# Half norms of a routed feed-forward query taken from its first product, with every engine's order of steps laid out anew

## The chip, the cores and the metric

The kernel runs on one core of one Trainium2 chip. The metric is the device time of one execution in microseconds (us). Before the change it was 1391.68 us, the median of 3 runs (1388.91 to 1394.45).

## The reference, cut to what matters

The input is 16 sequences of 375 steps with 64 channels. One layer is computed: a convolution over 9 steps with a norm-dependent scale and tanh (367 steps of 128 features are left), a banded attention with three window widths, and a feed-forward part that picks experts by product keys. The change is in the last:

```python
q = (hn @ Wq.T + bq).reshape(b, s, 8, 64)             # 8 heads of 64
mu, var = mean(q, -1), mean((q - mu) ** 2, -1)
q = (q - mu) / sqrt(var + 1e-5) * ln_g + ln_b
q0, q1 = q[..., :32], q[..., 32:]                     # two halves a head
s0 = l2norm(q0) @ l2norm(keys0).T                     # 64 keys each
s1 = l2norm(q1) @ l2norm(keys1).T
# top 16 of each, top 16 of the sums of pairs, softmax, experts ix0 + ix1
out = sum(gelu(hn . down[expert]) * w * up[expert])
```

So each tile needs, for each head, the variance of q and the squared norms of the two halves of the normalised q.

## The kernel before, in words

A sequence (batch) is worked in three tiles of 124 positions, t = 0, 1, 2. Each engine has a function `body(c)` that holds, in an order written out by hand, the steps it does in round c. The steps of a round belong to up to four batches: `do(step, c + k, t)` does the step for batch c + k, and nothing if there is no such batch. Engines meet through counting semaphores alone; every engine works strictly in the order of its own body. There are 20 rounds, c = -2 to 17. In `run`, rounds -2 to 3 are written out, rounds 4 to 13 are a hardware loop of five turns with two rounds each, and rounds 14 to 17 are written out again.

The steps around the change, for one tile:

- `q_product` (TensorE): q of the tile in bankQ, 124 positions x 512, one product of 512 columns plus a bias product from three rows (`fbq3`).
- `q_squares` (ScalarE): 8 squares with a running sum, one per head, give the variance (`qss`).
- `q_std` (GpSimd): adds eps, takes the root with a power, splits it in three bf16 parts (`std3`), and makes the guard. `q_turn_std` (TensorE) turns the parts, `q_stdT` (ScalarE) copies them.
- `q_second` (TensorE): a second product, with the gain in the weights (`wgT`) and the turned deviation times the bias: q times its deviation, 124 x 512 again.
- `q_norms` (ScalarE): 16 squares with a running sum, one per half, give `nss`. `q_guard` (VectorE) takes the larger of norm and guard, `q_scale` (GpSimd) its power -0.5.
- `q_score` (TensorE) computes 1024 key scores, `q_scores` (ScalarE) copies them, `rank` (VectorE) finds the top 16 of 16 x 64 values in four steps and two halves of the heads, `rank_sums` (GpSimd) adds pairs into 50 cells a head, `choose` (VectorE) takes the top 16 of these, and `mark`, `select`, `normalise`, `turn_cells`, `merge_cells`, `one_high`, `one_low`, `low_weights`, `scatter`, `product`, `experts_out`, `finish` turn them into the output of the tile.

Steps whose names begin with `p1_` are the convolution and attention of a later batch. `q_inner` and `q_gelu` (four each per batch) compute the experts' activations.

Set-up work stands in the first rounds: `turn_weights` (TensorE, round -1) waits for all feed-forward loads (`ffn_in`, L429), `key_norms`, `centred_weights`, `bias_parts` (VectorE, round -1) and `split_bias` (round 0) prepare weights and biases, `key_products` (TensorE, round 0) multiplies keys into weights, `send_parts` (the SP queue, L446) moves nine pieces of bias, and `copy_parts` (ScalarE, L734) copies them once they have landed. In VectorE's body the first step of a round is `p1_res` (L1434) and the second `product` (L1508).

Of the kernel before, what the change touches and what calls it, by code (L numbers as in the profile page):

```python
# [66 lines left out]
def build(nc, x, tok_kernel, tok_bias, wq, bq, wk, bk, wo, bo, gamma, beta, fwq, fbq, lng, lnb,  # L67
          keys0, keys1, down, up, merge, ident, own, out):
# [4 lines left out]
    with ctx:  # L73
# [21 lines left out]
        own_sb = sb("own_sb", [128, TG])  # L95
        ones = sb("ones", [128, 128])
        ones3 = sb("ones3", [3, NT], bf16)
# [129 lines left out]
        bankM = ctx.enter_context(nc.psum_tensor("bankM", [128, 1024], f32))  # L227
        wcT_ps = bankS[0:2 * NC, :].bitcast(f16).rearrange("p (k n) -> p k n", k=2)
# [10 lines left out]
        setup_fbq, fbq_spread = sem("setup_fbq"), sem("fbq_spread")  # L239
# [44 lines left out]
        qss_ready = sem("qss_ready")  # L284
# [3 lines left out]
        q2_done = sem("q2_done")  # L288
# [89 lines left out]
        def run(eng, start, body, end):  # L378

            start()  # L380
            for b in range(BEFORE, PEELED):
                body(Batch(b // 2, b % 2))
            with eng.Fori(PEELED // 2, B // 2 - 1) as j:
                body(Batch(j, 0))
                body(Batch(j, 1))
            for b in range(B - 2, AFTER):
                body(Batch(b // 2, b % 2))
            end()
# [10 lines left out]
                     (own_sb[:, :], own), (merge_sb[:, :], merge)]  # L399
# [6 lines left out]
        def _(sp):  # L406
# [24 lines left out]
            def spread():  # L431
# [3 lines left out]
                sp.wait_ge(setup_fbq, 5)  # L435
                for k in range(2):
                    sp.dma_start(fbq3[1 + k:2 + k, :], fbq_part[0:1, k, :]).then_inc(fbq_spread, 16)
# [11 lines left out]
            def body(c):  # L449
                if not at(c, -2):  # L450
                    do(load_x, c + 2)
                if at(c, -1):
                    spread()
                if at(c, 0):
                    send_parts()
                do(store, c + -2, 0)
# [12 lines left out]
        def _(pool):  # L469
# [226 lines left out]
        def _(act):  # L696
# [227 lines left out]
            def body(c):  # L924
# [47 lines left out]
                if at(c, -1):  # L972
                    copy_parts()
# [703 lines left out]
```

## Time and profile before

| | |
|---|---|
| median of 3 runs | 1391.68 us (1388.91 to 1394.45) |
| profiled execution | 1389.55 us, span 1387.7 us |
| VectorE (DVE) | 1284.9 us busy, 93% |
| TensorE (PE) | 1029.8 us, 74% |
| GpSimd (POOL) | 940.4 us, 68% |
| ScalarE (ACT) | 919.2 us, 66% |
| granted TensorE clock | 0.759 of full speed, mean |

The span is the time from the first to the last instruction of the profiled execution; what lies around it is 1.85 us. A busy time counts overlapping instructions of an engine once. "Idle before" is the time in which the engine did nothing before an instruction, with the instruction whose semaphore released it; "issue" means that no semaphore explains the wait. Because engines work in order, one late step delays all behind it on its engine.

### The profile page before, as it was taken

The page shows a single profiled execution, that of the slowest core. Times are in us where ns is not written, and L with a number is a line of the kernel's source. Part 1 is how long each engine was busy: PE and PEld are TensorE (multiplying, and loading weights), DVE is VectorE, ACT ScalarE, POOL GpSimd, SP SyncE. Part 2 cuts the span into 40 slices and gives each one's busy share as a digit, 9 for nine tenths or more (in the row PEclk, how much of TensorE's full clock was granted, in tenths as well). Part 3 has the DMA queues.
Part 4 walks back from the last instruction along what each step waited for, and adds up shares of the span by engine and source line. Part 5 has one row for each costly group of instructions (what it writes and reads, how often), then busy time and mean ns, then how long its engine had stood idle before and what let it go on. Part 6 is the DMA issues. An engine that isn't in the chain of part 4 may idle for free.

```text
span 1387.7 us, 41186 instructions
## 1 busy us (share of the span) xinstructions
PE 1029.8 (74%) x9585; PEld 679.4 (49%) x9585; DVE 1284.9 (93%) x10050; ACT 919.2 (66%) x4155; POOL 940.4 (68%) x1947
## 2 busy tenths in 40 slices
PE   4767777877777777778778777786778878776753
PEld 2434554645455454555446454553545545463433
DVE  4349999999999989999899998999999999999995
ACT  2576867668586857858576784767658676766532
POOL 4438776786867768577677867676776777668552
PEclk7787786769788776878877696787868778685555
DMA  2100000000000000000000000000000000000000
GB/s 55 18 15 2 3 11 3 4 8 6 10 4 11 4 5 11 4 10 4 12 4 5 9 6 10 4 12 3 5 9 5 6 3 5 4 4 5 3 4 7
DMA packets 22512, 10.97 MB, mean 8 GB/s; under 512 B 13920, under 2 KB 22032, under 8 KB 22242
## 3 DMA queue, kind: packets, MB, share of 16 engines
q1 hardware_dynamic: 21618, 7.79, 2.5%
q8 instruction: 82, 1.34, 0.4%
q14 instruction: 188, 1.54, 0.4%
q10 hardware_dynamic: 624, 0.30, 0.1%
HBM read 4.58 MB, written 3.01 MB: 5 GB/s over the span
## 4 chain that ended last, share of the span: by engine, by line
DVE 60%; issue 15%; PE 8%; ACT 7%; POOL 6%; SPq 1%; DVEq 1%; DMA 0%; POOLq 0%; ACTq 0%
DVE idx L1466 14%; DVE val L1464 9%; DVE cr L1536 8%; DVE scores L1469 8%; DVE oh L1479 6%; DVE best L1534 4%; DVE wl L1499 3%; ACT ns_junk L863 2%; PE banks L1055 2%; DVE bns L1389 2%; DVE masked L1419 1%; POOL cs L623 1%; PE bankM L1219 1%; PE bankQ L1142 1%; ACT act_g L840 1%
## 5 line engine op out<-in xcount | busy, mean ns | idle before, releaser
L1466 DVE FIND_INDEX8 idx<-val,scores 124x8 uint16<-124x64 f32 x1536 | 304.4, 216 | 0.0
L1464 DVE MAX8 val<-scores 124x8 f32<-124x64 f32 x1536 | 210.6, 207 | 2.4 <-ACT scores L870 1.2
L1219 PE MATMUL bankM<-wl,oh 128*128 128x16 f16 x5952 | 162.8, 172 | 46.2 <-DVE wl L1499 46.2
L1219 PEld LDWEIGHTS bankM<-wl,oh 128*128 128x128 f16 x5952 | 160.0, 101 | 59.6 <-DVE wl L1499 33.2
L597 POOL TENSOR_TENSOR qscale<-nmx,power 124x16 f32<-124x16 f32 x48 | 147.8, 3079 | 45.4 <-DVE nmx L1443 45.3
L1469 DVE MATCH_REPLACE8 scores<-val,scores 124x64 f32<-124x64 f32 x768 | 151.4, 206 | 0.0
L863 ACT ACTIVATE ns_junk<-bankQ 124x32 f32<-124x32 f32 x768 | 138.0, 255 | 12.7 <-PE bankQ L1172 12.4
L1479 DVE TENSOR_SCALAR oh<-eh 128x992 f16<-128x992 int16 x384 | 135.2, 414 | 4.5 <-ACT eh L918 4.5
L863 ACT ACTIVATION_READ_ACCUMULATOR ns_junk<-bankQ 124x1 f32 x768 | 138.3, 268 | 0.0
L1108 PE MATMUL banks<-diag,probs 124*124 124x124 f32 x672 | 107.7, 327 | 25.0 <-ACT diag L808 25.0
L1227 PE MATMUL bankM<-up_x,prod 128*124 128x128 f32 x384 | 86.5, 396 | 50.5 <-DVE prod L1508 50.5
L900 ACT ACTIVATE wcell<-wn 124x400 f16<-124x400 f32 x48 | 27.0, 562 | 142.0 <-POOL wn L648 142.0
L1108 PEld LDWEIGHTS banks<-diag,probs 124*124 124x124 f32 x672 | 100.3, 235 | 37.1 <-ACT diag L808 31.1
L1227 PEld LDWEIGHTS bankM<-up_x,prod 128*124 128x124 f32 x384 | 74.5, 287 | 76.8 <-DVE prod L1508 72.3
L623 POOL TENSOR_TENSOR cs<-val_s 124x64 f32<-124x64 f32 (+4 forms) x480 | 103.8, 250 | 7.5
L1466 DVE MATCH_VALUE_LOAD idx<-val,scores 124x8 f32 x1536 | 108.2, 70 | 0.0
L1182 PE MATMUL bankS<-wgk,hnT 128*124 128x512 f32 x192 | 105.3, 631 | 0.0
L1142 PE MATMUL bankQ<-hnT,down_x 128*128 128x372 f32 x128 | 74.0, 668 | 38.7 <-ACT ns_junk L863 22.4
L849 ACT ACTIVATE sq_junk<-bankQ 124x64 f32<-124x64 f32 x384 | 79.4, 238 | 31.6 <-PE bankQ L1156 31.3
L561 POOL TENSOR_TENSOR sbias<-smax,minus_scale 124x3 f32<-124x3 f32 x48 | 9.3, 195 | 133.0 <-DVE smax L1419 133.0
L1155 PE MATMUL bankQ<-fwqT,hnT 128*124 128x512 f32 x96 | 77.9, 905 | 14.5 <-ACT hnT L830 14.3
L586 POOL TENSOR_TENSOR std<-qvar,power 124x8 f32<-124x8 f32 x48 | 79.2, 1649 | 3.8
(196 smaller groups left out, 3067.8 us busy)
## 6 DMA issues: line engine op xcount, KB each, us to landing
x_in<-in_x SPq DMA_DIRECT2D x16, 93.8 KB
x_in<-in_x SPq DMA_DIRECT2D x16, 62.5 KB
out<-o_sb SPq DMA_DIRECT2D x16, 62.0 KB
out<-o_sb SPq DMA_DIRECT2D x16, 61.0 KB
out<-o_sb SPq DMA_DIRECT2D x16, 60.5 KB
x_in<-in_x SPq DMA_DIRECT2D x16, 31.0 KB
oh<-more SPq DMA_DIRECT2D x6, 54.0 KB
conv_w<-in_L_tok_kernel ACTq DMA_DIRECT2D x2, 128.0 KB, 3.2
```

The source lines that it names most:

```text
L597: g.tensor_tensor(qscale[c.slot(t)][:, :, :].rearrange("p h s -> p (h s)"), nmx[:, :, :].rearrange("p h s -> p (h s)"), power[0:NT, 0, :], ...
L623: g.tensor_tensor(dst[:, :, at:at + m], src[:, :, 0, a:a + 1].to_broadcast([NT, k, m]), src[:, :, 1, 0:m], ALU.add)
L863: last = a.activation(ns_junk[:, i, :], bankQ[0:NT, i * HALF:(i + 1) * HALF], ACT.Square, accum_out=nss[:, i // 2, i % 2:i % 2 + 1])
L1108: last = e.matmul(bankB[0:NT, k * NT:(k + 1) * NT], probs[t][w][:, OFF[k]:OFF[k] + NT], diag[:, w, :], start=w == windows[0], stop=w == wi ...
L1182: e.matmul(part, hnT[c.par][:, t, :], wgk[:, 2 * k:2 * k + 2, :].rearrange("p k n -> p (k n)"), start=True, stop=False)
L1219: last = e.matmul(coef[:, g, :, :], oh[:, k, g, :, :].rearrange("p v t -> p (v t)"), wl[:, part, k, :, TG * g:TG * (g + 1)], start=k + par ...
L1227: last = e.matmul(ffn, prod[:, l, :], up_x[:, l, :], start=l == 0, stop=l == EL - 1)
L1464: last = v.max(out=v_[:, hd, s, best8], in_=src[:, hd, s, :])
L1466: last = v.max_index(out=i_[:, hd, s, best8], in_max=v_[:, hd, s, best8], in_values=src[:, hd, s, :])
L1469: last = v.match_replace(out=src[:, hd, s, :], in_to_replace=v_[:, hd, s, best8], in_values=src[:, hd, s, :], imm_value=NEG)
L1479: last = v.tensor_scalar(by_shift[:, :, :, value, :], eh[:, :, :, :].rearrange("p s k (g t) -> p s (k g) t", t=TG), float(value), None, AL ...
L1536: last = v.match_replace(out=cr[:, hd, :], in_to_replace=best[:, hd, best8], in_values=left[:, hd, :], imm_value=NEG)
```

## The change

`q_product` gives q turned: four products with 128 rows of weights each, so that two heads' features lie on the partitions and the 124 positions are the columns. `q_squares` squares these four pieces, with the centred bias added on the way in (`q_lin[:, 16+k]`). A short product with six columns of weights then gives sums of the squares: two for the variances and four for the half norms, weighted with the gain squared. What is missing of a half norm is linear in q and in the deviation; `q_linear` computes it from four more weights per pair of heads (`q_lin[:, 0:16]`, and the first 16 columns of `bias96`). `q_nss` multiplies that by the deviation and adds it. A small matrix of block sums (`blocks`), the gain and the bias as columns are loaded: five loads more. `key_products` gets twelve short products, and the bias in three bf16 parts (`fbq3`, its two sends and five operations) goes.

The hardware loop goes: all 20 rounds are written out. The bodies of all engines are laid out anew.

```diff
         def run(eng, start, body, end):
             start()
-            for b in range(BEFORE, PEELED):
-                body(Batch(b // 2, b % 2))
-            with eng.Fori(PEELED // 2, B // 2 - 1) as j:
-                body(Batch(j, 0))
-                body(Batch(j, 1))
-            for b in range(B - 2, AFTER):
+            for b in range(BEFORE, AFTER):
                 body(Batch(b // 2, b % 2))
             end()
...
-                     (own_sb[:, :], own), (merge_sb[:, :], merge)]
+                     (own_sb[:, :], own), (blocks_sb[:, :], blocks), (merge_sb[:, :], merge)]
+        for i in range(2):
+            ffn_loads += [(gain_col[i * QD:(i + 1) * QD, :], col(lng)), (bias_col[i * QD:(i + 1) * QD, :], col(lnb))]
...
         # GpSimd
             def q_std(c, t):
...
-                link(g.tensor_tensor(qvar[:, :], qss[:, :], eps8[:, :], ALU.add))
...
+            def q_nss(c, t):
+                n = c.tile(t)
+                link = linker(pool, nss_ready, 2, n)
+                pool.wait_ge(sums_ready, n + 1)
+                pool.wait_ge(std_ready, 4 * n + 1)
...
+                link(g.tensor_tensor(by_pair(nlin[:, :, :]), lin, std, ALU.mult))
+                link(g.tensor_tensor(by_pair(nss[:, :, :]), by_pair(nlin[:, :, :]), squares, ALU.add), wait=False)
         # ScalarE
             def q_squares(c, t):
...
-                for i in range(H):
-                    last = a.activation(sq_junk[:, i, :], bankQ[0:NT, i * QD:(i + 1) * QD], ACT.Square, scale=QD ** -0.5, accum_out=qss[:, i:i + 1])
+                for k in range(PAIRS):
+                    last = a.activation(sqT[:, k * NT:(k + 1) * NT], bankQ[:, k * NT:(k + 1) * NT], ACT.Square, bias=q_lin[:, 16 + k:17 + k])
...
+            def q_var(c, t):
...
+                a.activation(qvar[:, :].rearrange("p (k h) -> p k h", h=2), q_sums_ps[:, :, 0:2], ACT.Identity, bias=eps8[:, 0:1]).then_inc(qvar_ready, 1)
...
-            def q_norms(c, t):
-                for i in range(2 * H):
-                    last = a.activation(ns_junk[:, i, :], bankQ[0:NT, i * HALF:(i + 1) * HALF], ACT.Square, accum_out=nss[:, i // 2, i % 2:i % 2 + 1])
+            def q_halves(c, t):
...
+                a.activation(half_sums[:, :, :], q_sums_ps[:, :, 2:10], ACT.Copy).then_inc(sums_ready, 1)
         # TensorE
             def q_product(c, t):
...
-                e.matmul(bankQ[0:NT, :], hnT[c.par][:, t, :], fwqT[:, :], start=True, stop=False)
-                e.matmul(bankQ[0:NT, :], ones3[:, :], fbq3[:, :], start=False, stop=True).then_inc(q_done, 1)
+                for k in range(PAIRS):
+                    last = e.matmul(bankQ[:, k * NT:(k + 1) * NT], fwqT[:, k * 128:(k + 1) * 128], hnT[c.par][:, t, :], start=True, stop=True)
+                last.then_inc(q_done, 1)
+            def q_sums(c, t):
+                n = c.tile(t)
+                pe.wait_ge(squared, n + 1)
+                for k in range(PAIRS):
+                    last = e.matmul(bankQ[0:NT, 10 * k:10 * k + 6], sqT[:, k * NT:(k + 1) * NT], q_sum_w[:, 0:6], start=True, stop=True)
+                last.then_inc(qsum_done, 1)
...
-            def q_second(c, t):
-                e.matmul(bankQ[0:NT, :], hnT[c.par][:, t, :], wgT[:, :], start=True, stop=False)
-                e.matmul(bankQ[0:NT, :], std96T[:, :], bias96[:, 0:H * QD], start=False, stop=True).then_inc(q2_done, 1)
+            def q_linear(c, t):
...
+                e.matmul(q_sums_ps[:, :, 6:10], hnT[c.par][:, t, :], by_pair(q_lin[:, 0:16]), start=True, stop=False)
+                e.matmul(q_sums_ps[:, :, 6:10], std96T[:, :], by_pair(bias96[:, 0:16]), start=False, stop=True).then_inc(lin_done, 1)
```

The new orders, where the prediction speaks of them (only the steps named):

```
TensorE, before:  ... p1_conv(c+1), p1_sum_sq(c+1), [round -1: turn_weights], q_turn_std(c-1,2) ...
TensorE, after:   ... [round -1: turn_weights], q_turn_std(c-1,2), q_linear(c-1,2), merge_cells(c-1,0), p1_conv(c+1), p1_sum_sq(c+1) ...
SP, before:       load_x(c+2), [round -1: spread], [round 0: send_parts], stores
SP, after:        [round -1: spread], [round 0: send_parts], load_x(c+2), stores
ScalarE, before:  ... q_squares(c+1,0), [round -1: copy_parts], ..., q_stdT(c+1,0), p1_ln(c+2,0), q_norms(c+1,0), [round -1: q_scores(0,0)], q_gelu(c+1,0), p1_xlT(c+2), ... q_gelu(c+1,1), ..., p1_qk(c+2) ...
ScalarE, after:   ... q_squares(c+1,0), best_exps(c,1), [round -1: copy_parts], mark(c,1), q_var(c+1,0), cell_exp(c,1), q_stdT(c+1,0), q_halves(c+1,0), ..., p1_ln(c+2,0), q_gelu(c+1,0), p1_xlT(c+2), ... q_gelu(c+1,1), ..., p1_qk(c+2), [round -1: q_scores(0,0)] ...
GpSimd, before:   rank_sums(c,0,0), rank_sums(c,0,1), ... normalise(c,2)
GpSimd, after:    q_nss(c,1), rank_sums(c,0,0), rank_sums(c,0,1), ... normalise(c,1), q_nss(c+1,0), ... normalise(c,2)
VectorE, before:  p1_res(c), product(c-2,2), p1_stats(c,1), ..., p1_moments(c,2), one_low(c-1,0), [round 0: split_bias], one_high(c-1,0), p1_shift(c,2), p1_wsq(c+1), ...,
                  rank(c-1,2,0,0), choose(c-1,1,0..3), ..., choose(c-1,2,0..3), one_high(c-1,1,0), p1_smax(c+1,0), one_low(c-1,1), one_high(c-1,1,1), ..., sum_exps(c,0), rank(c,1,0,0), rank(c,1,0,1), invert_sums(c,0)
VectorE, after:   p1_stats(c,1), invert_sums(c-1,0), p1_moments(c,1), rank(c-1,1,0,1), product(c-2,2), ..., choose(c-1,1,0), p1_shift(c,2), [round 0: split_bias], p1_wsq(c+1), ..., one_high(c-1,0), choose(c-1,1,2..3), rank(c-1,2,0,0), ...,
                  choose(c-1,2,0..2), p1_smax(c+1,0), one_high(c-1,1,0), one_low(c-1,1), one_high(c-1,1,1), choose(c-1,2,3), low_weights(c-1,1), ..., low_weights(c-1,2), p1_res(c+1), rank(c,1,0,0)
VectorE, batch 0: before rank(0,0,0,0..3), ..., p1_smax(1,0), p1_rden(1,0), p1_smax(1,1), p1_rden(1,1), p1_smax(1,2), rank(0,0,1,0..3)
                  after  p1_smax(1,0), ..., rank(0,0,0,0..3), p1_rden(1,0), p1_smax(1,1), p1_smax(1,2), p1_rden(1,1), rank(0,0,1,0..3)
```

## Rows read from the trace of the kernel before

**Rows 1.** The page: busy us (share of the span) and instructions.
```profile
PE 1029.8 (74%) x9585; PEld 679.4 (49%) x9585; DVE 1284.9 (93%) x10050; ACT 919.2 (66%) x4155; POOL 940.4 (68%) x1947
```

**Rows 2.** By stretch: length; PE, PEld, DVE, ACT, POOL busy; clock, DMA, GB/s.
```profile
113.70:432.65 318.95, 246.39 (x2379) 164.40 (x2379) 314.07 (x2500) 226.88 (x1036) 232.35 (x477) 0.79 0.02 6
432.65:1087.06 654.41, 504.17 (x4777) 336.15 (x4776) 630.88 (x5002) 455.22 (x2072) 464.21 (x952) 0.77 0.03 7
1087.06:1245.20 158.14, 122.91 (x1193) 82.37 (x1191) 157.16 (x1252) 113.26 (x516) 113.34 (x235) 0.79 0.02 4
1245.20:1387.70 142.50, 86.84 (x967) 55.16 (x965) 125.61 (x956) 65.75 (x299) 77.56 (x168) 0.57 0.02 5
```

**Rows 3.** DVE's waits, 432.65 to 1087.06: us in total, times, longest.
```profile
DVE res L1434 <- issue: 8.6, 4, 2.3
DVE prod L1508 <- issue: 7.4, 4, 1.9
```

**Rows 4.** Groups of ACT: output<-input xcount | busy us, mean ns | idle before.
```profile
L863 ACT ACTIVATE ns_junk<-bankQ 124x32 f32<-124x32 f32 x768 | 138.0, 255 | 12.7 <-PE bankQ L1172 12.4
L849 ACT ACTIVATE sq_junk<-bankQ 124x64 f32<-124x64 f32 x384 | 79.4, 238 | 31.6 <-PE bankQ L1156 31.3
L900 ACT ACTIVATE wcell<-wn 124x400 f16<-124x400 f32 x48 | 27.0, 562 | 142.0 <-POOL wn L648 142.0
```

**Rows 5.** Groups of PE, the same columns.
```profile
L1108 PE MATMUL banks<-diag,probs 124*124 124x124 f32 x672 | 107.7, 327 | 25.0 <-ACT diag L808 25.0
L1155 PE MATMUL bankQ<-fwqT,hnT 128*124 128x512 f32 x96 | 77.9, 905 | 14.5 <-ACT hnT L830 14.3
```

**Rows 6.** Groups of POOL, the same columns: the power and the splits of `q_std`.
```profile
L586 POOL TENSOR_TENSOR std<-qvar,power 124x8 f32<-124x8 f32 x48 | 79.2, 1649 | 3.8
L589 POOL TENSOR_TENSOR std<-std 124x9 f32<-124x9 f32 x96 | 19.3, 201 | 7.5
```

**Rows 7.** POOL in order of time, beside `split_bias`: start us, us, instruction.
```profile
58.12 1.61 POOL L554 TENSOR_TENSOR lnv<-bna,eps 124x3 f32<-124x3 f32 x1 [1.25 <-DVE bna L1399]
```

**Rows 8.** PE and DVE in order of time, 8 to 29 us.
```profile
8.30 6.09 PE L1055 MATMUL banks<-xT,conv_w 128*128 128x367 f32 x10 [0.95 <-ACT xT_sq L742]
14.32 0.81 PE L1064 MATMUL banks<-ones,sq_win 128*124 128x1 f32 x6
16.78 0.16 DVE L1366 TENSOR_SCALAR wsq<-banks 124x3 f32<-124x3 f32 x1
27.57 1.59 PE L1087 MATMUL banks<-xlT,wq_sb 128*128 128x367 f32 x2 [0.57 <-ACT xlT L779]
```

**Rows 9.** SP's queue in order of time: two of the loads.
```profile
11.85 0.37 SPq L429 DMA_DIRECT2D merge_sb<-in_merge  x1
12.27 2.42 SPq L429 DMA_DIRECT2D up_x<-in_L_ffn_expert_up  x4
```

**Rows 10.** DVE's waits, 0 to 113.7: us in total, times, longest.
```profile
DVE rden L1427 <- ACT probs L799: 13.5, 5, 3.7
DVE key_sq L1313 <- DMA up_x<-in_L_ffn_expert_up: 7.3, 1, 7.3
```

**Rows 11.** DVE and ACT in order of time, 49 to 86 us.
```profile
49.19 0.56 DVE L1434 TENSOR_TENSOR res<-banks,xb 124x384 f32<-124x384 f32 x1 [0.85 <-DVE key_z L1351]
72.28 1.48 ACT L734 ACTIVATE bias<-oh 96x1536 bf16<-96x1536 bf16 x1 [2.56 <-DMA oh<-more]
80.86 1.11 DVE L1464 MAX8 val<-scores 124x8 f32<-124x64 f32 x8 [1.17 <-ACT scores L870]
85.46 0.59 ACT L788 ACTIVATE kT<-banks,bk_sb 128x367 f32<-128x367 f32 x1
```

**Rows 12.** DVE in order of time, the last tile.
```profile
1365.34 0.20 DVE L1548 RECIPROCAL wrec<-wsum 124x8 f32<-124x8 f32 x1
```

**Rows 13.** ACT and POOL in order of time, a batch outside the loop.
```profile
1143.11 0.27 ACT L856 ACTIVATE std96T<-bankQ 96x124 bf16<-96x124 f32 x1 [0.74 <-PE bankQ L1162]
1150.02 0.40 POOL L617 TENSOR_TENSOR val_s<-val,qscale 124x128 f32<-124x128 f32 x1 [1.12 <-DVE val L1464]
```

More of the change, by code:

```diff
@@ L67, in build @@
 def build(nc, x, tok_kernel, tok_bias, wq, bq, wk, bk, wo, bo, gamma, beta, fwq, fbq, lng, lnb,
-          keys0, keys1, down, up, merge, ident, own, out):
+          keys0, keys1, down, up, merge, ident, own, blocks, out):
     f32, f16, bf16, i16, u16 = mybir.dt.float32, mybir.dt.float16, mybir.dt.bfloat16, mybir.dt.int16, mybir.dt.uint16
@@ L671, in body @@
                 do(q_std, c + 1, 0)
+                do(select, c, 1)
                 do(p1_rstd, c + 2, 0)
-                do(select, c, 1)
-                do(q_scale, c, 2)
+                do(normalise, c, 1)
                 if at(c, -2):
@@ L677, in body @@
                     setup_ffn()
[L678 removed]
+                do(q_nss, c + 1, 0)
+                do(p1_xb, c + 2)
                 do(rank_sums, c, 2, 0)
                 do(rank_sums, c, 2, 1)
+                do(rank_sums, c, 2, 2)
+                do(q_scale, c + 1, 0)
                 do(p1_sbias, c + 2, 0)
[L682 to L684 removed]
+                do(select, c, 2)
                 do(p1_sbias, c + 2, 1)
@@ L975, in body @@
                     copy_weights()
+                do(mark, c, 1)
+                do(q_var, c + 1, 0)
                 do(cell_exp, c, 1)
-                do(best_exps, c, 1)
-                do(mark, c, 1)
                 do(q_stdT, c + 1, 0)
+                do(q_halves, c + 1, 0)
+                do(weight_high, c, 1)
                 do(p1_ln, c + 2, 0)
-                do(q_norms, c + 1, 0)
-                do(weight_high, c, 1)
-                if at(c, -1):
-                    q_scores(c + 1, 0)
                 do(q_gelu, c + 1, 0)
@@ L1597, in body @@
                 do(rank, c + -1, 2, 1, 3)
+                do(choose, c + -1, 2, 0)
+                do(choose, c + -1, 2, 1)
+                do(choose, c + -1, 2, 2)
+                do(p1_smax, c + 1, 0)
+                do(one_high, c + -1, 1, 0)
+                do(one_low, c + -1, 1)
+                do(one_high, c + -1, 1, 1)
+                do(choose, c + -1, 2, 3)
+                do(low_weights, c + -1, 1)
+                do(sum_exps, c + -1, 2)
+                if at(c, -1):
+                    bias_parts()
                 if at(c, 0):
@@ L1668 @@
     given += [("merge", merge_matrix()), ("identity", np.eye(128, dtype=np.float32)),
-              ("own", np.tile(np.eye(TG, dtype=np.float32), (EH, 1)))]
+              ("own", np.tile(np.eye(TG, dtype=np.float32), (EH, 1))),
+              ("blocks", np.concatenate([np.kron(np.eye(2, dtype=np.float32), np.full((QD, 1), 1.0 / QD, np.float32)),
+                                         np.kron(np.eye(4, dtype=np.float32), np.ones((HALF, 1), np.float32)),
+                                         np.where(np.arange(128) < H, 0.5, 1.0).astype(np.float32)[:, None]], 1))]
     for name, a in given:
```

246 lines of the change are left out of this document (126 added, 120 removed).

## Prediction

> **What bounds the kernel now.** I read the page's busy shares first. VectorE (DVE) works in 93% of the span, the next engine in 74% [rows 1]. So the time is the DVE's work plus its holes, and a change that touches other engines is worth only the holes it fills or makes. The busy time by stretch shows where the holes are [rows 2]. Its borders are the starts of `res`, one per batch.
> - 1087.06 to 1245.20: two batches from written-out code, 79.07 us each, of which the DVE works 78.58. That is the floor of a batch; nothing in the change shortens it.
> - 113.70 to 432.65: four batches at the start of the full pipeline, 79.74 each.
> - 432.65 to 1087.06: eight batches in which the loop's four jumps back lie, 81.80 each. 654.41 - 8 x 79.07 = 21.9 us is lost here.
> - 1245.20 to the end: 142.50, with 16.9 of holes, nearly all in the last tile's chain.
> - Before 113.70 the DVE works about 57 us (1284.9 less the four rows), so it stands still for about 56.
>
> The waits inside the loop stretch [rows 3] name the loss: `res` 8.6 us and `prod` 7.4 us, four times each, released by "issue", by nothing that a semaphore shows. They come in pairs, at the first two steps of the loop body, about 4 us a jump. Neither stands in the written-out stretches. The other 5.9 us (21.9 - 16.0) are short waits after the jumps, while the other engines, which stood still too, catch up.
>
> **The change, part by part.**
> 1. *Loop written out.* It removes the four jumps. The batches then cost what written-out ones cost in this trace: -21.9 us. Bounds: the named holes alone (-16.0), or all thirteen later periods at 79.07, which adds 4 x 0.67 (-24.6). I take 21.9. More code could bring holes of its own; the two written-out stretches on either side of the loop have the same density of instructions and no "issue" wait over 0.3 us, so I put nothing on it.
>
> 2. *ScalarE (ACT).* Out go 8 squares and 16 half norms per tile, at 238 and 255 ns plus an accumulator read each [rows 4]; in come 4 squares of 124 columns and two small copies. The 124 columns lie between 238 ns (64) and 562 ns (400 columns) [rows 4], say 0.3. The removed pieces overlap their reads, so ACT loses less than their sum of 8 x 0.24 + 16 x 0.26 = 6 us a tile, and gains some 2. On the path this is worth 0 in the steady state, as the DVE waits there for almost nothing; it buys slack for the new orders.
>
> 3. *TensorE (PE).* The product becomes 4 weight blocks in two fp32 passes, 8 x 0.327 by the 124-column row, against 2 x 0.905 and the bias product [rows 5]: about equal. The second product gives way to some ten short passes. PE is at 74% and off the path: 0.
>
> 4. *GpSimd (POOL).* One small operation goes, two come, about 0.2 us each [rows 6]: +0.2 us x 48 = 10 us on an engine with 447 us free. Direct cost 0; indirect, DVE and POOL can block each other. While the DVE splits the bias, a POOL addition took 1610 ns [rows 7] against 200 for an ordinary small one. Here POOL was the one that waited. For the other direction the bounds are 0 and 10 us (each of the 48 extra operations holds the DVE up in full); the row shows POOL as the loser, so I stay near 0: +0.3.
>  The Trainium skill ("SBUF — State Buffer", Who interferes with whom) says that a DVE instruction with two SBUF inputs and a POOL one that reads SBUF exclude each other for the whole instruction, and the loser waits. The trace agrees with the rule on the row just named. By the rule's worst case the sum would be 10 us higher, 1392; by the row, 1382.
>
> 5. *The order at the start.* This is the part that costs. `p1_conv` of the first batch now stands behind `turn_weights` in PE's queue, and `turn_weights` waits for all feed-forward loads. Before, the convolution ran at 8.30 to 14.39, inside the loading, and the DVE took `wsq` at 16.78 [rows 8]. Now:
>  - five more loads stand ahead of `up_x` in SP's queue. One costs about 0.4 to 0.6 us to issue (0.37 for `merge_sb`, 2.42 for the four of `up_x` [rows 9]); 5 x 0.475 = 2.4. `key_sq`, which waited 7.3 us for the last load [rows 10] and started at 16.29, comes at 18.7.
>  - five transposes, 0.9, then the convolution: 6.09 as now [rows 8]; on a PE that has stood still since 7.4 it may run at the lower clock throughout, 0.80 a pass as in `L1087` [rows 8], so up to 8.0. Then 0.81 for the window sums.
>  - 18.7 + 0.9 + 6.1 + 0.8 = 26.5, and `wsq` at 26.6: +9.8 us. Bounds: 7.3 (convolution at a full-clock 3.6) and 11.7. Nothing hides it, since the DVE has nothing else to do but the two key norms; all of batch 0 hangs on `wsq`.
>
> 6. *The first scores.* Times here are without the 9.8. `split_bias` moves behind the last shift, about 1.6 us later, so the nine sends and `copy_parts`, now at 72.28 [rows 11], come at 74.0. `q_var`, which now stands behind `copy_parts` in ACT's queue, starts the chain (power 1.65 and splits of 0.2 [rows 6], turn, copy, linear part, halves, sums) only at 75.5, where it ran beside the sends before. Sums at 80.6. Then ACT takes `q_scores(0,0)` only after two GELUs and `p1_qk(1)`: k lies at 85.46 today [rows 11] and comes about 2.5 later, 88.1, so scores at 89.1 in place of 80.7 (first MAX8 at 80.86 [rows 11]). The DVE fills part of it: it used 5.7 + 1.2 + 3.7 + 2.9 us of waits between 73.8 and 97.5 anyway. Laid out anew (mask 0 at 89, ranking to 96.5, mask 1, then mask 2 behind the exponentials of tile 1) it is where it was at 97.5 at about 101.3: +3.8. Bounds: 0 (the waits for the exponentials, 13.5 in all [rows 10], swallow it) and 8.9 (89.8 - 80.9, nothing filled).
>  `bias_parts` shrinks by some 2.8 us of DVE work, but `res(0)`, which started at 49.19 after 0.85 us of waiting [rows 11], hangs on the attention output: 0.
>
> 7. *Other moves in the steady state.* Each waits for something with room: `res` ahead of the ranking, `choose` of tile 1 ahead of the marks, `smax` ahead of `one_high`. I value the lot at 0, from -2.7 (the four early periods fall to 79.07) to +7 (half a us of new wait a batch).
>
> 8. *Tail.* Before, `wrec` at 1365.34 released the last chain [rows 12]. The last `choose` step now stands behind the one-hot work of tile 1, so `mark` and `select` come some 2 us later and end just behind `wrec`: +0.5, between -1 and +3.
>
> Sum: -21.9 + 0.3 + 9.8 + 3.8 + 0.5 = -7.5. The profiled execution took 1389.55 (span 1387.7, 1.85 around it), which gives 1382.0. It lies 2.1 us under the median of the runs shown, within their spread; I add half of that: **1383**.
>
> **Rivals.**
> - *A. The start costs little* (the convolution stays at the full clock or its lateness is taken up by the DVE's other waits, and the first scores find cover): half of 13.6 or less is lost. For it: 56 us of waits there, some of which could shrink. Against it: they hang in one chain. Loop gain and early periods in full: 1389.6 - 24.6 + 6 = 1371 to 1376. Say 1374.
> - *B. POOL's queue takes the place of the jumps (slower).* `q_nss(c,1)` stands at the head of POOL's list, ahead of the cell sums that `choose(c,0)` waits for. It hangs on `q_halves`, `q_linear`, `q_turn_std`. In a straight batch POOL waited 1.12 us for the DVE at the second cell sums, at 1150.02 [rows 13]; that and about 0.5 is the slack. The transposed deviation was copied at 1143.11 [rows 13], so the halves can lie at 1147 and POOL is free of `normalise` only at 1147.6: no wait. It decides from the point where the halves come after 1148.1. Each us beyond costs 1 us in 14 batches. At 1.2 us beyond: 1382 + 17 = 1399.
> - *C. It comes out even.* Gain 16 to 18 (only the named holes), start 13 to 15, and a few tenths a batch of new waits: 1389.6 - 17 + 14 + 3 = 1389.6, or 1390 as a median.
> - *D. The jump holes don't go* (they belong to the first steps of a body, not to the jump): 1389.6 + 14 = 1404. Against it: `res` and `prod` show no such wait in written-out bodies (the four waits are those of 4 of 16 `res`) [rows 3].
>
> **How the numbers follow.** Chances: forecast (1379 to 1387) 0.49, A 0.20, B 0.08, C 0.20, D 0.03. About 7 us (0.5%) is what can be told from no change here: faster means under 1384.7, slower over 1398.6. Of the forecast's own case some three quarters lie under 1384.7: 0.37 + 0.20 from A = 0.57, and 0.01 of C: 0.58. Slower: B's upper half and D, with a little of C's tail: 0.08. The rest, 0.34, is within. Range: from A's 1371 to just short of B: 1371 to 1397.
>
> **What would show it.** In the profile after: no "issue" waits of 2 us before `res` or `prod`, and `res` every 79 to 79.5 us throughout (step 1); the convolution of batch 0 at about 19.6 behind the weight turns and `wsq` at 26 to 29 (step 5); the first MAX8 of the rankings at about 99 to 101 in place of 80.86 (steps 5 and 6); ACT busy for well under 850 us. The prediction is wrong if periods stay over 80 us (then look at `best <- cs` and `nmx <- nss` for B), or if the first ranking starts before 93.

## The result, and the profile after

The changed kernel took **1369.63 us** (median of 5, 1369.41 to 1369.84); the kernel before, beside it, 1393.53. The ratio is 0.983, 95% interval 0.982 to 0.985: 23.9 us faster. The forecast was 1383, 8.7 under the 1391.68 it started from, and the measured time lies below the stated range. The profiled spans fell by 20.0 us, 1387.7 to 1367.7.

The page's busy line after (against [rows 1]):
```profile
PE 1025.0 (75%) x10233; PEld 793.4 (58%) x10233; DVE 1265.5 (93%) x10048; ACT 779.1 (57%) x2141; POOL 940.1 (69%) x1994
```
The stretches after between starts of `res`, as in [rows 2]:
```profile
123.53:437.38 313.85, 247.54 (x2420) 192.32 (x2418) 310.00 (x2499) 193.62 (x536) 232.59 (x490) 0.74 0.02 6
437.38:1065.63 628.25, 500.55 (x5088) 390.34 (x5088) 621.40 (x5001) 385.05 (x1064) 462.95 (x977) 0.75 0.03 7
1065.63:1222.32 156.69, 124.05 (x1269) 97.58 (x1269) 155.50 (x1252) 95.50 (x264) 113.16 (x242) 0.75 0.02 4
1222.32:1367.70 145.38, 84.75 (x1135) 65.20 (x1135) 128.08 (x997) 52.83 (x127) 82.87 (x174) 0.56 0.02 5
```
Every stretch of full batches has nearly one pitch (the time from one `res` to the next): 78.46, 78.53 and 78.35 us a batch, where before they had 79.74, 81.80 and 79.07. The start grew by 9.8 us (123.53 against 113.70), the last stretch by 2.9.

This border flatters the start, because `res` has moved in the DVE's order: ahead of `res(1)` the DVE now issues 305 instructions where it issued 347, and behind the start of `res(15)` 997 where it issued 956. A step of batch 1 that stands well behind that border, its first `nmx`, comes 12.7 us later (before, then after):
```profile
151.11 0.15 DVE L1443 TENSOR_TENSOR nmx<-nss,qguard 124x16 f32<-124x16 f32 x1
```
```profile
163.82 0.17 DVE L1482 TENSOR_TENSOR nmx<-nss,qguard 124x16 f32<-124x16 f32 x1
```
From the first `nmx` of the last batch to the end it is 107.6 us before and 106.8 after. So the start lost 12.7 us, the 14 batches won 31.9, and the tail is about as long as it was.

Idle time of the DVE is about what it was (102.2 us in the span, 102.8 before: the jumps' holes went, the start's came, 73.0 in place of 56.5 ahead of `res(1)`). What fell is its **busy** time, by 19.4 us. Only 2.8 of that was forecast.

The whole steady state, `res(1)` to `res(15)`, 14 batches, in one row: before first, then after (behind the length: PE, PEld, DVE, ACT, POOL).
```profile
113.70:1245.20 1131.50, 873.47 (x8347) 582.92 (x8346) 1102.12 (x8750) 795.35 (x3624) 809.91 (x1664) 0.78 0.03 6
```
```profile
123.53:1222.32 1098.79, 872.13 (x8777) 680.24 (x8775) 1086.90 (x8749) 674.17 (x1864) 808.71 (x1707) 0.75 0.02 6
```
The DVE issues the same number of instructions (8750, 8749) and is busy with them for 15.2 us less. Its groups say where; the shift `lnm` of before, then of after:
```profile
L1406 DVE SCALAR_TENSOR_TENSOR lnm<-bna,lnr 124x3 f32<-124x3 f32 x48 | 14.4, 300 | 7.5 <-POOL lnr L555 7.5
```
```profile
L1445 DVE SCALAR_TENSOR_TENSOR lnm<-bna,lnr 124x3 f32<-124x3 f32 x48 | 7.7, 161 | 13.5 <-POOL lnr L551 13.5
```
Three columns took 0.76 us in the batch of before that is shown next. In order of time, the DVE's `lnm` and what follows it, and POOL's `wsel` beside them:
```profile
1114.82 0.76 DVE L1406 SCALAR_TENSOR_TENSOR lnm<-bna,lnr 124x3 f32<-124x3 f32 x1
1115.51 0.66 DVE L1508 TENSOR_TENSOR prod<-bankM,act_g 128x496 f32<-128x496 f32 x1
...
1114.62 0.95 POOL L641 TENSOR_TENSOR wsel<-taken,cx 124x400 f32<-124x400 f16 x1
```
`lnm` ends with `wsel` (1115.58 and 1115.57). In 11 of the 16 batches of before, the first `lnm` took 0.52 to 0.87 us and ended within 0.02 us of `wsel`. After, `select` stands ahead of the inverse deviation in POOL's order and `lnm` two ranking steps later on the DVE; beside the one at 1101.12 POOL is idle, and it takes 0.16 us, 0.06 to the next start. None takes over 0.25.

The start, DVE and PE after, against [rows 8, 10]:
```profile
19.62 0.22 DVE L1355 TENSOR_TENSOR key_sq<-key_in 64x64 f32<-64x64 f32 x1 [10.65 <-DMA up_x<-in_L_ffn_expert_up]
27.08 0.16 DVE L1405 TENSOR_SCALAR wsq<-banks 124x3 f32<-124x3 f32 x1 [6.99 <-PE banks L1093]
...
20.77 5.46 PE L1084 MATMUL banks<-xT,conv_w 128*128 128x367 f32 x10
26.15 0.81 PE L1093 MATMUL banks<-ones,sq_win 128*124 128x1 f32 x6
```
The convolution runs behind the weight turns, and `wsq` comes 10.3 us later than before. The first ranking starts behind batch 1's first mask, which waits:
```profile
98.20 0.30 DVE L1458 CUSTOM_DVE_ANT_0 masked<-banks,mask 124x136 f32<-124x136 f32 x1 [7.94 <-PE banks L1126]
...
99.02 0.60 DVE L1503 MAX8 val<-scores 124x8 f32<-124x64 f32 x4
```

### The profile page after: what moved, and what is told of

Its sections match the earlier page's. It is cut to its first block, busy times and chain, and to the rows that moved or that the text cites. A ratio compares the mean times of both kernels' runs of the same rounds, so it can differ in the third digit from the quotient of the medians.

```text
span 1367.7 us, 38641 instructions
## 1 busy us (share of the span) xinstructions
PE 1025.0 (75%) x10233; PEld 793.4 (58%) x10233; DVE 1265.5 (93%) x10048; ACT 779.1 (57%) x2141; POOL 940.1 (69%) x1994
## 4 chain that ended last, share of the span: by engine, by line
DVE 55%; issue 14%; PE 12%; ACT 9%; POOL 7%; SPq 2%; DMA 0%; DVEq 0%; POOLq 0%; ACTq 0%
DVE idx L1505 14%; DVE val L1503 9%; DVE scores L1508 8%; DVE cr L1575 6%; DVE oh L1518 5%; PE banks L1084 5%; DVE best L1573 3%; DVE wl L1538 2%; ACT act_g L855 2%; PE bankM L1266 2%; ACT probs L814 1%; DVE bns L1428 1%; DVE masked L1458 1%; POOL wsel L650 1%; ACT eh L939 1%
## 5 line engine op out<-in xcount | busy, mean ns | idle before, releaser
L1505 DVE FIND_INDEX8 idx<-val,scores 124x8 uint16<-124x64 f32 x1536 | 312.2, 247 | 0.0
L1505 DVE MATCH_VALUE_LOAD idx<-val,scores 124x8 f32 x1536 | 155.3, 101 | 0.1
L1191 PE MATMUL bankQ<-q_sum_w,sqT 128*124 128x6 f32 x384 | 76.0, 324 | 74.3 <-ACT sqT L863 74.3
L1191 PEld LDWEIGHTS bankQ<-q_sum_w,sqT 128*124 128x124 f32 x384 | 71.9, 282 | 80.6 <-ACT sqT L863 80.6
L1137 PE MATMUL banks<-diag,probs 124*124 124x124 f32 x672 | 116.8, 346 | 1.0 <-ACT diag L823 1.0
L1137 PEld LDWEIGHTS banks<-diag,probs 124*124 124x124 f32 x672 | 114.1, 261 | 2.1 <-ACT diag L823 1.2
L648 POOL TENSOR_TENSOR wcell<-taken,ce 124x400 f16<-124x400 f16 x48 | 49.6, 1033 | 86.5 <-issue 86.4
L1266 PEld LDWEIGHTS bankM<-up_x,prod 128*124 128x124 f32 x384 | 76.1, 286 | 31.3 <-DVE prod L1547 22.7
L1171 PE MATMUL bankQ<-hnT,down_x 128*128 128x372 f32 x128 | 79.8, 716 | 18.4 <-ACT act_g L855 13.8
L582 POOL TENSOR_TENSOR std<-qvar,power 124x8 f32<-124x8 f32 x48 | 79.1, 1648 | 9.9 <-ACT qvar L871 8.7
L1084 PE MATMUL banks<-xT,conv_w 128*128 128x367 f32 (+1 forms) x160 | 84.3, 685 | 0.0
L939 ACT ACTIVATE eh<-bankM,digit_bias 128x248 int16<-128x248 f32 x192 | 74.0, 475 | 14.9 <-PE bankM L1243 14.8
## 6 DMA issues: line engine op xcount, KB each, us to landing
x_in<-in_x SPq DMA_DIRECT2D x16, 62.5 KB
```

Of the source, the lines that this page charges most:

```text
L1084: last = e.matmul(bankB[:, 0:T], conv_w[0:k, m, :], xT[0:k, 2 * m:2 * m + T], start=m == 0, stop=m == 4)
L1137: last = e.matmul(bankB[0:NT, k * NT:(k + 1) * NT], probs[t][w][:, OFF[k]:OFF[k] + NT], diag[:, w, :], start=w == windows[0], stop=w == wi ...
L1191: last = e.matmul(bankQ[0:NT, 10 * k:10 * k + 6], sqT[:, k * NT:(k + 1) * NT], q_sum_w[:, 0:6], start=True, stop=True)
L1266: last = e.matmul(ffn, prod[:, l, :], up_x[:, l, :], start=l == 0, stop=l == EL - 1)
L1505: last = v.max_index(out=i_[:, hd, s, best8], in_max=v_[:, hd, s, best8], in_values=src[:, hd, s, :])
```

## The experiments

Times are medians; the kernel before had 1390 to 1393 in each comparison. The kernels are called e1 to e18, and where an expectation counts them, it counts so (the ninth experiment is e9). *Theory P* of the expectations: loop, start and collisions on the SBUF port between DVE and POOL explain the result. By the *port* it means a path to SBUF, the memory on the chip that both engines work from, which they would have to share, so that one holds the other up. "A batch" is (start of `res(15)` - start of `res(1)`) / 14.

**A. Only the loop written out, e1** (`for b in range(BEFORE, AFTER)` in the kernel before).

> The kernel before with its loop written out, nothing else. Theory P (the jumps cost what their holes showed; the lower floor comes from the new orders, which keep GpSimd's reads of SBUF off VectorE's two-input instructions): 21.9 us less than before, 1371.7 beside a median of 1393.5, batches of 79.0 to 79.2 us. Rival L (writing out lowers the floor by itself): 30 us less, 1363, batches at 78.5. Rival M (the lower floor comes from the new maths): as P, 1371.7.

1373.18 us, -18.5 (ratio 0.9875, 0.985 to 0.990); span 1371.4, -16.3.
```profile
113.95:1228.80 1114.85, 871.10 (x8347) 580.63 (x8346) 1101.07 (x8749) 791.38 (x3624) 809.73 (x1664) 0.78 0.02 6
```
Against the row of before almost only idle time went (29.4 to 13.8 us). The expectation was 21.9 us; 3.4 of them did not come. Most batches take 79.1, but four take 80.8 to 81.2 though there is no jump; their holes are these waits:
```profile
DVE oh L1474 <- ACT eh L913: 5.3, 4, 1.4
```
So part of the 5.9 us which the forecast called catching up after jumps belongs to the old order. The floor of a batch stays at 79.1: writing out alone does not lower it.

**B. Orders alone, maths alone.** In e4 the written-out kernel gets all new orders of POOL, ACT, PE and DVE, with `q_second` and `q_norms` where `q_linear` and `q_halves` stand; in e5 the new maths stands in the old orders (but for SP's: old in e4, new in e5). Cut from e5, against e1:
```
 do(q_product, c, 0)
+do(q_sums, c, 0)
...
-do(q_second, c, 0)
+do(q_linear, c, 0)
```


> Loop written out and the new orders, but before's second query product and half norms on ScalarE. Theory P: batches of 78.4 to 78.6 us as in the changed kernel, the start 8 us later than in the kernel before (convolution behind the weight turns), 1369 to 1372. Rival M (the maths shortens the batch): batches of 79.1, 1377 to 1380. If before's longer ScalarE work turns into waits in these orders: above 1380.

> Loop written out and the new maths, in before's orders (the sums behind the product, the half norms' linear part where the second product stood; the convolution ahead of the weight turns). Theory P: batches of 79.0 to 79.2 us, VectorE's normalising shift still at 300 ns, start as before or up to 3 us earlier, 1366 to 1372. Rival M: batches at 78.5, 1360 to 1364. If the longer chain of the new maths makes waits in the old orders: above 1375.

1446.05 and 1487.20 us: 73 and 114 **more** than e1. Stretch and first waits in it, e4, then e5:
```profile
127.00:1296.27 1169.27, 877.65 (x8226) 587.91 (x8224) 1097.99 (x8748) 796.57 (x3630) 797.02 (x1664) 0.77 0.02 6
DVE wsum L1537 <- ACT best_exp L883: 24.2, 14, 1.8
DVE best L1529 <- POOL cs L624: 11.1, 14, 0.8
```
```profile
123.77:1338.62 1214.85, 893.88 (x8889) 689.68 (x8890) 1101.92 (x8749) 664.21 (x1860) 838.25 (x1706) 0.73 0.02 6
DVE nmx L1482 <- POOL nss L599: 47.1, 14, 3.4
DVE el L1525 <- ACT expert L941: 22.1, 14, 2.2
```
83.5 and 86.8 us a batch; what they take more than e1 is idle time of the DVE (71.3 and 112.9 us in the 14 batches, against 13.8). The new orders wait most for ACT, which still works 797 us in the stretch; the new maths, whose norms go PE-ACT-PE-ACT-POOL, waits most for POOL's `nss` in the old orders. As built here, neither half has a value of its own. Whether a half would have one in orders tuned for it was not tested.

**C. The convolution first, e3.** In the changed kernel, PE's order for the first batch alone:
```
 if at(c, -1):
+    p1_conv(c + 1)
+    p1_sum_sq(c + 1)
     turn_weights()
```


> The changed kernel with the first batch's convolution ahead of the weight turns in TensorE's queue, as it was before the change. Theory P, by the prediction's step 5: wsq at 17 us in place of 27.1, all behind it 7.3 to 9.8 us earlier, 1360 to 1362 beside 1369.6. Rival A (the start's lateness is taken up by other waits): under 4 us, 1366 to 1369.

1362.07 us, 7.6 less than the changed kernel; `key_sq` at 19.15, `wsq` right behind it at 19.65 (the expected 17 forgot that the key norms stand ahead of it in the DVE's order), batches still 78.49.

**D. The added loads last, e8**, on a semaphore of their own (`late_in`), on top of that.

> The changed kernel with the convolution first, and its five added loads sent last, on a semaphore of their own that only the two users wait for. By the prediction's step 5 (five issues of 0.475 us ahead of up_x) key_sq and wsq come 2.4 us earlier: 1359.7 beside 1362.1. If the added loads are swallowed by other transfers: no change, 1362.

1360.08 us, 2.0 less; `key_sq` at 16.73, 2.4 us earlier. Both parts of step 5 together are 9.6 us.

**E. The first scores, e9 and e10.** On ACT, on top of e8:
```
 do(q_stdT, c + 1, 0)
+if at(c, -1):
+    copy_parts()
 do(q_halves, c + 1, 0)
```
and `q_scores(0,0)` ahead of `q_gelu(0,0)`.

> As the one before, and on ScalarE the first tile's deviation is copied ahead of copy_parts, and its scores ahead of the first GELU. By the prediction's step 6: lnm of batch 1 no longer waits 9.4 us behind GpSimd's q_std, the first ranking starts 6 to 9 us earlier, and 3.8 us (0 to 8.9) come back: 1355.9. If the first scores only trade one wait of the start for another: 1359 to 1360.

1360.94 us: nothing. `lnm` of batch 1 waits 2.4 us in place of 9.2, but the mask behind it waits 13.6, and the ranking starts at 91.23 (90.15 in e8). In the changed order the DVE takes batch 1's mask ahead of the ranking, so earlier scores alone bring nothing: it waits for batch 1's attention, and TensorE's score product (4.3 us) now stood in front of that.

> As the ninth experiment, but the first tile's scores go behind the turn of xl in TensorE's queue and behind its copy in ScalarE's, and VectorE takes the first ranking ahead of batch 1's first mask, which waited 13.6 us there. Theory: the ranking (7.7 us) starts at about 83.5 us in place of 91.2 and fills that wait; res of batch 1 comes 4 to 8 us earlier and the time is 1353 to 1357 beside 1360.9. Rival (the whole start hangs on batch 1's attention, so it is no use to rank earlier): 1359 to 1361.

1357.11 us, 3.8 less than e9 and 3.0 less than e8. Here the ranking fills the wait, from 83.05 on. Ranking first, then batch 1's mask, is also how the kernel before had it: e3, e8 and e10 together give back 12.5 us (1369.63 to 1357.11) of the 12.7 that the change cost at the start.

**F. Single moves, e6, e7, e11.** In e6 `select(c,1)` ahead of `p1_rstd(c+2,0)` in e1's kernel (below), in e7 the reverse in the changed one, in e11 only the DVE's shift `p1_shift(c+1,0)` two steps later, in e1's:
```
-do(p1_rstd, c + 2, 0)
 do(select, c, 1)
+do(p1_rstd, c + 2, 0)
```


> The kernel before, written out (the first experiment), and one swap in GpSimd's order: select of tile 1 ahead of the inverse deviations of the next batch's first normalisation, as in the changed kernel. Theory P (a VectorE instruction with two inputs in SBUF stands still for as long as a GpSimd one reads SBUF; the shift lnm used to land on wsel): lnm of that normalisation falls from 0.8 us to 0.06, the batch from 79.1 to about 78.5, the time by 8 to 10 us against 1373.2. Rival M (the lower floor has nothing to do with GpSimd's order): lnm unchanged or its gain lost to another wait, 1372 to 1374.

> The changed kernel with that swap undone (select of tile 1 behind the inverse deviations). Theory P: lnm back at 0.7 to 0.8 us in most batches, the batch at 79.0 to 79.3 in place of 78.5, the time 8 to 10 us longer, 1377 to 1380. Rival M: 1369 to 1371.

> The kernel before, written out, and only VectorE's shift of the next batch's first normalisation moved two ranking steps later (GpSimd's order untouched). Theory P: lnm then no longer meets wsel, 0.8 us becomes 0.06 and, unlike with the swap in GpSimd's order, no wait for the inverse deviation takes its place: the undisturbed batch falls from 79.1 to 78.4, the time by 8 to 10 us, 1363 to 1365 beside 1373.2. Rival (what is saved comes back as waits for the one-hot input, as with the swap): 1371 or more.

1385.14 (+12.0), 1401.65 (+32.0) and 1406.24 us (+33.1). `lnm` fell and rose as P says (7.5, 12.1 and 7.1 us in all, against 15.0, 7.7 and 15.0; in e7 it took 0.50 us in 14 batches, where 0.7 to 0.8 was expected), but the times did not follow. DVE's waits in the 14 batches, in the order of the runs:
```profile
DVE lnm L1401 <- POOL lnr L550: 12.0, 14, 1.2
DVE oh L1474 <- ACT eh L913: 9.1, 8, 1.3
```
```profile
DVE oh L1518 <- ACT eh L939: 15.2, 14, 1.1
DVE masked L1458 <- PE banks L1126: 10.7, 10, 1.3
```
```profile
DVE best L1529 <- POOL cs L624: 21.4, 28, 1.3
DVE oh L1474 <- ACT eh L913: 12.3, 14, 1.7
```
In e6 the 0.8 us at the port came back as 0.86 us a batch of waiting for the inverse deviation, which now stands behind `select`. One move in an order tuned as a whole costs 0.8 to 2.3 us a batch; it says little about the mechanism it was meant to test.

**G. Reads and writes of POOL, e12 and e13.** On top of e3: four extra instructions a batch where POOL is idle, beside `el`, `ol` and `oh`; `tensor_tensor(probe_out, probe_in, probe_in)` in e12, `memset(probe_out)` in e13.

> The changed kernel with the convolution first (1362.1), and on GpSimd, where it stood idle, four extra products of two tiles in SBUF (124x400, 0.95 us each) a batch, whose result nobody uses. Theory P: VectorE's two-input instructions beside them (ol 0.60, wl 1.17 us) stand still for up to one such product each: ol and wl of that tile 0.3 to 1 us longer, the batch 0.8 to 1.6 us, the time 1373 to 1387. Rival (engines do not hinder each other, the order is what counts): 1361 to 1363.

> The control to the one before: the same four places, but fills that only write (124x1088, about 0.95 us each). Theory P: nothing reads, so nothing is held up: 1361 to 1364. If it is the length of GpSimd's work that counts and not its reads: as the one before.

1399.06 and 1409.07 us: the control cost more than the test, and both cost more than theory P's 1373 to 1387 and 1361 to 1364. DVE and POOL in order of time, with reads, then with writes:
```profile
969.93 3.08 POOL L614 TENSOR_TENSOR qscale<-nmx,power 124x16 f32<-124x16 f32 x1
971.58 1.39 DVE L1530 TENSOR_SCALAR oh<-eh 128x992 f16<-128x992 int16 x4
...
972.89 0.22 DVE L1537 TENSOR_SCALAR el<-expert 128x248 int16<-128x248 int16 x1
973.14 1.22 DVE L1541 TENSOR_TENSOR ol<-el,lows 128x992 f16<-128x992 int16 x1
974.29 3.36 DVE L1530 TENSOR_SCALAR oh<-eh 128x992 f16<-128x992 int16 x4
...
972.98 4.06 POOL L580 TENSOR_TENSOR probe_out<-probe_in 124x400 f32<-124x400 f32 x4
```
```profile
978.29 1.10 DVE L1537 TENSOR_SCALAR el<-expert 128x248 int16<-128x248 int16 x1
979.43 0.67 DVE L1541 TENSOR_TENSOR ol<-el,lows 128x992 f16<-128x992 int16 x1
980.02 3.38 DVE L1530 TENSOR_SCALAR oh<-eh 128x992 f16<-128x992 int16 x4
...
978.05 4.76 POOL L580 MEMSET probe_out<- 124x1088 f32 x4
```
`ol`, with two SBUF inputs, stretches beside a read (1.22) and not beside a write (0.67, as ever). `oh`, one input and 16 bits wide, stretches beside **both** (3.4 us for four, 1.4 elsewhere), and so does `el` where it starts beside a probe (here in e13: 1.10; in e12 it started before the probe). The Trainium skill ("SBUF — State Buffer", Who interferes with whom) has both rules: a DVE instruction with two SBUF inputs contends with a POOL one that reads SBUF and not with one that only writes, and the DVE's two-port modes, which `tensor_scalar` can enter, contend with POOL, the loser waiting for the whole instruction. Beside the probes the trace agrees with each; that `oh` runs in such a mode no row says. My expectation had forgotten the second.

The trace does not agree for every POOL instruction. `qscale`, a power of 16 columns, ran for 3.08 us beside four `oh` (first two rows), and they took 1.39 us. In e3, 224 `oh` beside `qscale` took 0.33 us each to the next start and 14 `ol` took 0.59, as without a neighbour. So two instructions side by side are not yet a stall; the long duration is the sign.

What these stalls cost can be read from the 14 batches, e12, then e13 (e3: 1098.91 long, DVE busy 1086.99):
```profile
118.45:1248.63 1130.18, 863.12 (x8777) 672.12 (x8776) 1122.63 (x8748) 674.71 (x1864) 864.34 (x1763) 0.75 0.02 6
115.87:1255.23 1139.36, 872.96 (x8777) 673.95 (x8775) 1127.37 (x8748) 674.52 (x1860) 872.27 (x1763) 0.74 0.02 6
```
35.6 us more of busy time made e12's batches 31.3 us longer, 40.4 made e13's 40.5 longer. Stalls of this size cost nearly all that they last.

**H. One instruction, e14 and e15.** On top of e3: one probe a batch behind `wn`, so that it lies beside `lnm`; a read in e14, a write in e15.

> The changed kernel with the convolution first (1362.1), and one extra GpSimd product of two tiles in SBUF (124x400, 0.95 us) a batch, put where GpSimd stood idle for 0.65 us, beside VectorE's lnm of the next batch's first normalisation (0.06 us now). Theory P: lnm takes 0.7 to 0.8 us again, as before the change, the batch 79.2 in place of 78.5, and the time is 1372 to 1374. Rival (VectorE is not held, only GpSimd's queue gets 0.3 us later): 1362 to 1366 with lnm at 0.06.

> The control: at the same place a GpSimd fill of 124x1088, which took about 1.1 us and only writes. Theory P: lnm, with two inputs, is not held by a write and stays at 0.06 us: 1362 to 1365 (a little for GpSimd's later queue). If writes hold it too: 1372 to 1376.

The read, then the write:
```profile
1014.36 0.62 DVE L1457 SCALAR_TENSOR_TENSOR lnm<-bna,lnr 124x3 f32<-124x3 f32 x1
...
1014.11 0.85 POOL L579 TENSOR_TENSOR probe_out<-probe_in 124x400 f32<-124x400 f32 x1
```
```profile
1014.51 0.14 DVE L1457 SCALAR_TENSOR_TENSOR lnm<-bna,lnr 124x3 f32<-124x3 f32 x1
...
1014.24 1.00 POOL L579 MEMSET probe_out<- 124x1088 f32 x1
```
So the port holds `lnm`: 13.7 us in all with the read, 7.0 with the write, and in all 14 batches it ends within 0.02 us of the probe. But the times are 1363.38 and 1361.99, and the batch 78.51 and 78.47: for 6.7 us of stall the kernel pays 1.4 (0.6 in the 14 batches of the profiles), less than the runs of either spread (2.3 and 2.7). Theory P's size, 10 us, fell for this stall. The wait before `wsq` shrank from 8.6 us to 0.9, so most of the stall could go where the DVE would have waited for PE. That is not the only reading: PE's granted clock was also higher with the read, in every run (0.768 to 0.772, against 0.732 to 0.748), and a faster PE could shorten the same wait. The two were not separated.

**I. What sets 78.5?** On top of e10, the `up_x` loads also late (e16), then `wsq` behind `low_weights` on the DVE (e17), or the convolution ahead of `merge_cells` on PE (e18).

> As the tenth experiment (1357.1), with the four up_x loads also on the later semaphore, so that VectorE's key norms wait only for what they use. key_sq comes at about 14.5 us in place of 17.1; wsq then hangs on the convolution alone (window sums done at about 15.1): 2 to 2.5 us earlier, 1354.6 to 1355.1. If something else sets wsq: 1357.

> As the last experiment (1354.9), but VectorE takes low_weights of tile 0 (1.17 us) ahead of wsq, which waits up to 1 us a batch for TensorE's window sums. If VectorE's work bounds the batch and that wait is a hole in it: the batch falls from 78.5 to 78.0, 1348 to 1351. If a ring over TensorE bounds it: the wait appears elsewhere and the time stays at 1354 to 1356. If tscale or q_guard then come too late for the tanh: above 1357.

> As e16 (1354.9), but TensorE takes the next batch's convolution and window sums (7 us) ahead of the merge of tile 0's cells, for which it waits 0.67 us. If the ring goes over the convolution and wsq: the wait before wsq goes and the batch falls to 78.0, 1348 to 1351. But the merge comes 7 us later, and with it the one-hot input of tile 0: if that has less room than 7 us, waits before oh take its place and the time is above 1360.

1354.91, 1355.04 and 1359.46 us. e16 is the fastest kernel of the study (ratio to before 0.973, 0.972 to 0.975). In e17 and e18 the wait for `wsq` is gone and others stand in its place; the waits of 14 batches:
```profile
DVE nmx L1493 <- POOL nss L603: 3.4, 14, 0.3
```
```profile
DVE el L1536 <- ACT expert L946: 9.4, 14, 3.4
```
The batches stay at 78.36 and 78.69. What sets the pitch stays open: the DVE's busy time is near it (77.6 us a batch), but adding 6 us of it (e14) left it where it was, and taking a wait away (e17, e18) did not lower it.

**J. The loop again, e2**, in the changed kernel.

> The changed kernel, but batches 4 to 13 in a hardware loop again, two per pass, as before the change. By step 1 (21.9 us in the old kernel; taking the loop out of it brought 18.5): 1388 to 1392, with two waits of about 2 us a pass that nothing explains. If the new orders are hit less by a jump: 1380 to 1386.

1382.49 us, 12.9 more than without it. The waits of 14 batches name where it shows now:
```profile
DVE o_sb L1559 <- PE bankM L1271: 8.7, 4, 2.4
DVE best L1578 <- POOL cs L643: 4.4, 4, 1.1
```
Four times each, once a jump, but on other engines' account: in the new body the jump shows on PE and POOL, not as "issue" on the DVE. POOL's own wait, which the changed kernel does not have (PE's `bankQ` at L1213 has one like it, 10.2 us in four):
```profile
POOL nlin L603 <- issue: 8.1, 4, 2.1
```

## Why the prediction was wrong

The spans fell by 20.0 us; in the prediction's steps:

- *What bounds the kernel: "the floor of a batch; nothing in the change shortens it"*, and with it **step 7, valued at 0 (-2.7 at best). This is the step that failed.** From e1 to the changed kernel the 14 batches lose 16.1 us: 14.2 of DVE busy time, 1.9 of idle. I read 78.58 us of busy time as work. Some of it was standing at the port. By the groups of the whole run, e1 and then the changed kernel: `lnm` 15.0 and 7.7 us, `wl` 62.5 and 60.3, `tscale` 3.9 and 3.2, some 10 us together. In e1 twelve `wl` took 0.87 us, beside POOL's cell sums as here; in the changed kernel none takes over 0.70:
```profile
1086.57 1.45 DVE L1494 TENSOR_TENSOR wl<-wm,ol 128x992 f16<-128x992 f16 x2
1087.57 1.35 POOL L618 TENSOR_TENSOR cs<-val_s 124x64 f32<-124x64 f32 x5
```
  `oh` fell by 2.4 and `ol` by 0.5, `nmx` and `prod` rose by 1.0 and 0.5; these were not traced to a neighbour. The rows that show it (`lnm` with three columns at 300 ns) were in the trace of before; I looked only at [rows 7], where POOL is the loser, and asked what POOL's **new** operations would add, not what the new order takes apart. That the orders do this is shown: with them and the old maths `lnm` and `wl` have 7.2 and 60.3 us (e4), though the DVE's busy time in e4's 14 batches, in all, is only 3.1 us under e1's. What the stalls are worth is not shown: `lnm`'s, put back, cost about a fifth of its length (e14, under a higher clock), larger ones nearly all of theirs (e12, e13). How much of the 16.1 they carry stays open.
- *Steps 2 and 3 at 0, "it buys slack for the new orders"*: ACT's busy time fell by 140 us, 2.9 a tile, where about 4 were forecast. The sentence fits what came, and the value followed from pricing parts one by one. Without the new maths the new orders take 83.5 us a batch; which part of it they need was not separated, but their longest wait is for ACT (24.2 us). The right reading is one term for maths and orders together, and its rows (which waits the ACT ends in the new order) don't exist in a trace of before.
- *Step 1, -21.9*: -18.5 in the old orders (spans -16.3), nearest to the bound of the named holes, 16.0. The 5.9 us of small waits did not all go. In the new orders the loop is worth 12.9.
- *Step 4, +0.3*: POOL's busy time is the same (940.4, 940.1), where 10 us more were forecast, and the DVE's busy time fell, so the ten us of the worst case did not come.
- *Step 5, +9.8*: right in mechanism and, by some luck, in size: `key_sq` came at 19.62 and not 18.7, the convolution took 5.46 us and not 6.09. Forecast `wsq` at 26.6, measured 27.08; undone, it gives 7.6 + 2.0 back. Rival A, whose time was the nearest, was wrong in its reason.
- *Step 6, +3.8*: right in the main. The first ranking came at 99.02, as said (99 to 101). The point that was to move from 97.5 to 101.3 (the second half of tile 0's ranking) came at 109.80, which is 2.5 us beyond the start's 9.8; by the first `nmx` of batch 1 it is 2.9 (12.7 less 9.8). In `res(1)`, 9.8 us later, this does not show, as `res` moved ahead of work that it stood behind. The cause was only half named: early scores alone give nothing back (e9), early scores with the ranking ahead of batch 1's mask give 3.0 us (e10 against e8).
- *Step 8, +0.5*: the last stretch grew by 2.9, of which the idle part is 0.4 (17.3 against 16.9); the rest is DVE work that the earlier `res` now leaves behind the border. By `nmx` the tail is 0.9 shorter. Within its bounds.
- *Rivals*: B did not come (`nmx` waits 0.8 us for POOL once). D fell: `res` and `prod` show no wait for "issue". C had the loop (16 to 18) and nearly the start (13 to 15) and failed where the forecast did, on the batch. Of the signs, `res` every 79 to 79.5 us is the one that did not come: it was 78.4 to 78.5.

The forecast's sum with step 1 at -16.3 and step 7 at -16.1 would be 1389.55 - 16.3 + 0.3 + 9.8 + 3.8 - 16.1 + 0.5 = 1371.6, against 1369.7 in the profiled execution; every term but step 7 held within its bounds.

## What to carry to other kernels

Busy time isn't work: before calling a pitch a floor, look for short instructions with long means, and lay the other port user's instructions beside them. A stall in front of a wait can vanish in it (e14); others cost their length (e12, e13). When a change moves the step that you measure from, measure from a second one as well. A rewrite of maths and orders is one term; test it as a whole, and expect a single moved step of a tuned order to cost. In the start, ask which queue the first chain stands in: putting the convolution, the late loads and the first ranking right gave 14.7 us (1369.63 to 1354.91), of which the first 12.5 (to e10) give back what the change had cost there.

## What the runs showed of the hardware

- A POOL `memset` of 1 us, which reads nothing, held 16-bit `tensor_scalar`s of the DVE (four `oh`: 1.4 to 3.4 us) and left a two-input `tensor_tensor` alone (0.67). A POOL product of 400 columns held both kinds (3.4 and 1.22 us). A POOL power of 16 columns held neither (four `oh` 1.39 us beside it in e12, `ol` 0.59 to the next start in e3).
- A held `lnm` ended within 0.02 us of its POOL neighbour: 11 of 11 in the kernel before, 14 of 14 in e7 and in e14.
- A taken jump of the loop cost 4.6 us in the old body (18.5 / 4) and 3.2 in the new one (12.9 / 4). Why they differ was not tested.
- PE's granted clock over the 14 batches was 0.75 in e15 and 0.79 in e14, which differ by one POOL instruction a batch. Over whole runs it was 0.732 to 0.748 in the five of e15 and 0.768 to 0.772 in the five of e14. PE was busy 29 us less in e14, and the batch was the same. What moved the clock wasn't tested. The two rows, e15 first:
```profile
115.83:1214.43 1098.60, 872.41 (x8777) 680.54 (x8775) 1086.82 (x8748) 672.89 (x1864) 818.76 (x1721) 0.75 0.02 6
```
```profile
115.94:1215.13 1099.19, 843.57 (x8777) 652.52 (x8775) 1092.84 (x8749) 671.53 (x1864) 816.84 (x1721) 0.79 0.02 6
```
